# Output and score banks that rotate, and the old output copied in two pieces, in the head loop of an attention layer

## The chip, the cores and the metric

The kernel runs on one core of a Trainium2 chip. The metric is the device time of one execution in microseconds (us), as the median of several runs. The engines are PE (TensorE: matmuls; its weight loads are shown as PEld), DVE (VectorE), ACT (ScalarE), POOL (GpSimd) and SP (SyncE, which issues the DMAs here).

## What is computed

One post-norm transformer layer on x of shape (4, 2048, 256), with 16 heads of 16 channels, rotary positions, and an FFN with int weights and hidden size 768:

```python
qkv = x @ w_qkv + b_qkv
q, k = _rope(q), _rope(k)
attn = softmax(q @ k.T / sqrt(16))          # per batch and head, 2048 x 2048
out = (attn @ v) @ w_out + b_out
x = _layernorm(x + out)
wg, wu, wd = w_gate / 127, w_up / 127, w_down / 127
x = _layernorm(x + (silu(x @ wg.T) * (x @ wu.T)) @ wd.T)
```

## The kernel before

There are three stages: `project` (queries, keys and values, rotary positions), `attend` (the head loop, 80% of the time) and `finish` (output projection, norms, FFN). The change is in `attend` and in `keep`, a step on the SP queue.

`attend` goes over 64 heads (4 batches of 16). Its work on one head h:

- *Maxima.* For softmax each query row needs its largest score. PE computes scores (`scores`, `score_half`, L91) of 128 queries by 1024 keys into one of two tiles `s_ps` (two PSUM banks each); a tile g is computed in halves j = 0 and 1, called scores A and B here. DVE takes the maximum of each tile (`tile_maximum`, L102). There are 32 tiles a head, and they run ahead: while head h is in the loop, its step n computes tile g = (h + 1) * 32 + 10 + n. Tile g waits until DVE has read tile g - 2 (semaphore `s_read`). Of two tiles a head (in steps 10 and 24), ACT copies the first 512 columns to `spared` (L1038) for POOL to fold, and DVE reads only the other 512.
- *Exponentials.* PE computes transposed scores (`scores_t`, L942): product e of 64 in a head (key tile e // 4, 512 queries e % 4), one bank each, called st(e) here. The rows of q hold the maxima, so the product comes out with the maximum taken off. There are ST = 3 banks `st_ps`; product n (counted over all heads) goes to bank n % 3 and waits until exponential n - 3 is done (`exp_done`). ACT takes the exponential into `probs` (L1063).
- *Times v.* `times_v` (L953, called PV here) multiplies probs of a key tile by v (16 channels and a column of ones, so the sum of the exponentials comes with it). It accumulates over the head's 16 key tiles into one bank, `o_ps`. It is issued in halves of 256 queries per key tile, each of four column groups; an fp32 matmul is recorded as two passes, so a half shows as 8 matmuls.
- *Drain.* When the last PV of head h - 1 is done, ACT copies `o_ps` to `sums` in SBUF (`drain`, L1032), behind exponential 4 of head h, and SP stores it (`keep`). The first PV of head h waits for that copy (`sums_out`).

The order on PE is written out in one loop. In each step n = 0 to 31 of head h it issues scores A, st(2n), scores B, one half of PV, and st(2n + 1). So st(2n + 1) runs beside scores A of the next step (they use different rows of the array), and st(2n + 2) beside scores B. PV trails by three steps: steps 0 to 2 issue the last three halves of head h - 1, and step 3 the first half of head h. In the last head the odd st goes ahead of PV.

The order on ACT is exponentials 0, 1, 2, ..., with the drain behind exponential 4 and the copies to `spared` behind exponentials 20 and 48. On SP, a head's turn is: the second stacks of head h + 1, `keep` of head h - 1 (four small DMAs of the sum's row to `spread`, then four stores to `heads`), the first stacks of head h + 2, the inverses of head h - 1 (after DVE's reciprocal at L745, which is issued behind the tile of step 10), and the maxima of head h + 1. The banks in `attend` are 4 for `s_ps`, 3 for `st_ps` and 1 for `o_ps`, all 8.

The functions that the change touches:

Of the kernel before, what the change touches and what calls it, by code (L numbers as in the profile page):

```python
# [7 lines left out]
P = 128  # L8
# [3 lines left out]
BANK = 512  # L12
# [20 lines left out]
def wait(eng, sem, value):  # L33

    if not isinstance(value, int) or value > 0:
        eng.wait_ge(sem, value)
# [687 lines left out]
def unit_steps(t, u, T, D):  # L724

    HD = D // N_HEAD
    QC = T // BANK
    PQ = P // QC

    def keep(sp, h):  # L730

        i = h % 2
        sp.wait_ge(u["sums_out"], h + 1)
        wait(sp, u["inverses_out"][i], h // 2 * 16)
        for c in range(QC):
            sp.dma_start(u["spread"][i][c * PQ:(c + 1) * PQ, :],
                         u["sums"][i][c * 32 + HD:c * 32 + HD + 1, :].rearrange("o (p n) -> o p n", p=PQ)
                         ).then_inc(u["spread_in"][i], 16)
        for c in range(QC):
            sp.dma_start(t["heads"][h * HD:(h + 1) * HD, c * BANK:(c + 1) * BANK],  # L740
                         u["sums"][i][c * 32:c * 32 + HD, :]).then_inc(u["kept"][i], 16)

    def invert(dve, h):
        dve.wait_ge(u["spread_in"][h % 2], (h // 2 + 1) * QC * 16)
        dve.reciprocal(u["spread"][h % 2][:, :], u["spread"][h % 2][:, :]).then_inc(u["inverted"], 1)  # L745

    def inverses(sp, h):
        sp.wait_ge(u["inverted"], h + 1)
        sp.dma_start(t["inverses"][h:h + 1, :].rearrange("h (p n) -> (h p) n", p=P), u["spread"][h % 2][:, :]
                     ).then_inc(u["inverses_out"][h % 2], 16)  # L750

    return dict(keep=keep, invert=invert, inverses=inverses, **u)


def attend(nc, t, w, s, f, u, B, T, D):

    HD = D // N_HEAD
    HEADS = B * N_HEAD
    KT = T // P
    QC = T // BANK  # L760
    QT = T // P
    EXPS = KT * QC
    HALF = BANK // 2
# [5 lines left out]
    ST = 3  # L769
    RING = 4  # L770
# [3 lines left out]
    VM = HD + 1  # L774
# [15 lines left out]
    LEVELS = 9  # L790
    FOLDS = 3 * LEVELS
    LOWEST = -3.0e38
    with ExitStack() as ctx:  # L793
        def sb(name, shape, dt=F32):
            return ctx.enter_context(nc.sbuf_tensor(name, shape, dt))

        def psum(name, shape):
            return ctx.enter_context(nc.psum_tensor(name, shape, F32))
# [5 lines left out]
        out = unit_steps(t, u, T, D)  # L804
        q, k, first_in, second_in = s["q"], s["k"], s["first_in"], s["second_in"]
        probs = [sb(f"probs{i}", [P, T]) for i in range(RING)]
# [5 lines left out]
        larger = sb("larger", [P, BANK // 2])  # L812
        more_top = sb("more_top", [P, QT])
        max_parts = [sb(f"max_parts{i}", [P, PARTS, 32], F16) for i in range(2)]
        st_ps = [psum(f"st_ps{i}", [P, BANK]) for i in range(ST)]
        o_ps = psum("o_ps", [P, BANK])
        TT, KD = WIDE // D, D // P
        p_first = [s_ps[c][:, :].rearrange("p (n d) -> p n d", n=TT) for c in range(2)]

# [4 lines left out]
        o_cleared = sem("o_cleared")  # L824
# [13 lines left out]
        exp_done = sem("exp_done")  # L838
        pv_done = sem("pv_done")
        sums_out, kept, inverses_out = out["sums_out"], out["kept"], out["inverses_out"]  # L840
        spread_in = out["spread_in"]
# [74 lines left out]
        def _(pe):  # L916
# [12 lines left out]
            def scores_t(h, e):  # L929

                if e == 0:
                    pe.wait_ge(second_in[h % 2], (h // 2 + 1) * SECOND_DMAS * 16)
                    pe.wait_ge(max_in[h % 2], (h // 2 + 1) * PARTS * 16)
                kt, c = e // QC, e % QC
                n = h * EXPS + e
                rows = SECOND
                if h == HEADS - 1 and e % 2 == 1:
                    rows = FIRST
                    if e == 1:
                        pe.wait_ge(low_in, (SECOND_DMAS + PARTS) * 16)  # L940
                wait(pe, exp_done, n - ST + 1)
                pe.matmul(st_ps[n % ST][:, :], k[h % 2][rows, kt * P:(kt + 1) * P],  # L942
                          q[h % 2][rows, c * BANK:(c + 1) * BANK], start=True, stop=True).then_inc(st_done, 1)

            def times_v(h, kt, half):

                if half == 0:
                    pe.wait_ge(exp_done, h * EXPS + (kt + 1) * QC)
                    if kt == 0:
                        wait(pe, sums_out, h)  # L950
                at = half * HALF
                for c in range(QC):
                    mm = pe.matmul(o_ps[c * 32:c * 32 + VM, at:at + HALF], t["kept"][:, h, kt, :],  # L953
                                   probs[(h * KT + kt) % RING][:, c * BANK + at:c * BANK + at + HALF],
                                   start=(kt, half) == (0, 0), stop=(kt, half) == (KT - 1, 1), tile_position=(0, c * 32))
                if half == 1:
                    mm.then_inc(pv_done, 1)
# [22 lines left out]
            for g in range(EARLY + 2, MAXES + LEAD):  # L980
                scores(g, 0)
                scores(g, 1)
                if g == MAXES // 2:
                    pe.wait_ge(b_spread, D // P)
                    pe.wait_ge(out_in, 3 * 16)
                    for kd in range(D // P):
                        mm = pe.matmul(st_ps[0][:, 0:D], w["b_v"][:, kd, :], w["w_out"][:, kd, :], start=kd == 0,
                                       stop=kd == D // P - 1)
# [3 lines left out]
            for h in range(HEADS):  # L992
                for n in range(EXPS // 2):
# [9 lines left out]
                    before, half = divmod(n - 3, 2)  # L1003
# [12 lines left out]
        @block.scalar  # L1016
        def _(act):
            act.wait_ge(out_in, 3 * 16)
            act.wait_ge(all_ones, 1)
            for kd in range(D // P):  # L1020
                act.activation(w["b_v"][:, kd, :], w["ones"][:, :], ACT.Identity,
                               scale=w["b_v_cols"][:, kd:kd + 1]).then_inc(b_spread, 1)
            act.wait_ge(ffn_in, len(FFN) * 16)
            for name in FFN:
                act.copy(w[name][:, :, :], w[name][:, :, :].bitcast(I32)).then_inc(floats, 1)

            def drain(h):
                i = h % 2
                act.wait_ge(pv_done, (h + 1) * KT)
                wait(act, kept[i], h // 2 * QC * 16)  # L1030
                wait(act, spread_in[i], h // 2 * QC * 16)
                act.copy(out["sums"][i][:, :], o_ps[:, :]).then_inc(sums_out, 1)  # L1032

            def keep_half(n):

                act.wait_ge(half_done, n + 1)
                wait(act, folded, FOLDS * n)
                act.copy(spared[:, :], s_ps[SPARED[n] % 2][:, 0:BANK]).then_inc(half_kept, 1)  # L1038

            def beside(n):  # L1040

                if n == KEEP_WIDE:
                    act.wait_ge(f["wide_summed"], 1)
                    act.copy(f["wide_count"][:, :], s_ps[0][:, 0:1]).then_inc(f["wide_known"], 1)
                    act.wait_ge(f["wide_known"], 1)
                    act.copy(f["wide_int"][:, :], f["wide_count"][0:1, :]).then_inc(f["wide_known"], 1)
                if n in TAKE_HIGH:
                    steps["take_high"](act, 0, TAKE_HIGH.index(n))
                if n in TAKE_WHOLE:
                    steps["take_whole"](act, 0, TAKE_WHOLE.index(n))  # L1050

            scale = act.alloc_register("exp_scale")
            for h in range(HEADS):
                if h % N_HEAD == 0:
                    b = h // N_HEAD
                    act.reg_load(scale, s["exp_scale"][0:1, b:b + 1].bitcast(I32))
                for e in range(EXPS):
                    kt, c = e // QC, e % QC
                    if c == 0:
                        wait(act, pv_done, h * KT + kt - RING + 1)  # L1060
                    n = h * EXPS + e
                    act.wait_ge(st_done, n + 1)
                    act.activation(probs[(h * KT + kt) % RING][:, c * BANK:(c + 1) * BANK], st_ps[n % ST][:, :],  # L1063
                                   ACT.Exp, scale=scale).then_inc(exp_done, 1)
                    if e == QC and h > 0:
                        drain(h - 1)
                    g = (h + 1) * MAXES + LEAD + e // 2
                    if e % 2 == 0 and g in SPARED:
                        keep_half(SPARED.index(g))
                    if h == HEADS - 1 and e % 2 == 1:  # L1070
                        beside(e // 2)
            steps["load_silu"](act)
            drain(HEADS - 1)

        @block.vector
        def _(dve):
            def clear():
                dve.memset(o_ps[:, :], 0.0).then_inc(o_cleared, 1)
                for i in range(2):
                    dve.memset(head_top[i][:, :], 0.0).then_inc(cleared, 1)  # L1080
                    dve.memset(tile_max[i][:, :, KW:KW + 1], LOWEST).then_inc(cleared, 1)

# [513 lines left out]
```

## Time and profile before

| | |
|---|---|
| time, median of 3 runs (lowest, highest) | 2868.82 us (2866.64, 2869.18) |
| span of the profiled execution, first to last instruction | 2868.1 us |
| part of the span before, in and behind the head loop | 240, 2306, 322 us |
| PE, DVE, ACT, POOL busy, of the span | 98%, 94%, 90%, 49% |
| drains L1032, each | 64, 0.59 us |
| exponentials L1063, each | 4096, 0.60 us |

The profile is of one execution. Its own time is the span of 2868.1 us and what lies around it; the profile gives no other time for it, and the median of the runs is 0.7 us above the span. Busy time counts an instruction from its recorded start to its end, and instructions of one engine overlap, so a busy share near 100% doesn't say that the engine could do no more.

### The profile page before, as it was taken

To read this page: it belongs to the slowest core of one execution; us is meant where nothing else is said; L and a number is where in the kernel's file an instruction comes from. 1 tells how busy PE (TensorE), PEld (TensorE's weight loads), DVE (VectorE), ACT (ScalarE), POOL (GpSimd) and SP (SyncE) were. 2 spreads that over 40 slices of the span, in tenths; PEclk is the share of its full clock that TensorE was granted. 3 is DMA by queue.
4 is the path that set the end of the run, shared out by engine and by line. 5 is a ranking of instruction groups with operands and counts; after the bars stand their busy time and mean duration, and the time that the engine had idled before them with its cause. 6 is when DMAs were issued, how large, how long until landed. Compare 5 with 4: busy or idle time off the path is not lost. (4 is left out here: it accounts for less than half of the span.)

```text
span 2868.1 us, 70575 instructions
## 1 busy us (share of the span) xinstructions
PE 2811.7 (98%) x27022; PEld 862.5 (30%) x27022; DVE 2702.9 (94%) x3088; ACT 2591.9 (90%) x4778; POOL 1416.7 (49%) x4133
## 2 busy tenths in 40 slices
PE   8989999999999999999999999999999999999998
PEld 4531222222222222222222222222222222246665
DVE  7989999999999999999999999999999999947777
ACT  5756999999999999999999999999999999976555
POOL 7851444444444444444444444444444444436553
PEclk9978999999999999999999999999999999999999
DMA  5431111111111111111111111111111111233431
GB/s 194 142 116 28 36 35 36 35 36 35 35 35 35 34 35 36 35 36 36 35 35 35 36 35 35 35 35 36 35 35 36 35 35 35 70 90 92 118 96 38
DMA packets 121519, 146.56 MB, mean 51 GB/s; under 512 B 52832, under 2 KB 87520, under 8 KB 121180
## 3 DMA queue, kind: packets, MB, share of 16 engines
q1 hardware_dynamic: 120892, 142.02, 17.0%
q8 instruction: 214, 3.51, 0.5%
q14 instruction: 125, 1.02, 0.1%
q10 hardware_dynamic: 288, 0.01, 0.0%
HBM read 106.30 MB, written 35.13 MB: 49 GB/s over the span
## 5 line engine op out<-in xcount | busy, mean ns | idle before, releaser
L102 DVE TENSOR_REDUCE tile_max<-s_ps 128x1 f32<-128x1024 f32 (+1 forms) x2048 | 2282.4, 1185 | 8.8 <-PE s_ps L91 2.8
L1063 ACT ACTIVATE probs<-st_ps 128x512 f32<-128x512 f32 x4096 | 2202.2, 601 | 71.0 <-PE st_ps L942 41.1
L953 PE MATMUL o_ps<-probs,kept_v 128*17 128x256 f32 x16384 | 1283.1, 385 | 25.7 <-ACT sums L1032 25.7
L91 PE MATMUL s_ps<-k,q 64*128 64x512 f16 x4096 | 1266.2, 386 | 11.0 <-DVE tile_max L102 9.2
L942 PE MATMUL st_ps<-q,k 64*128 64x512 f16 x4096 | 1249.5, 382 | 1.1 <-ACT probs L1063 0.8
L1198 POOL TENSOR_TENSOR larger<-spared 128x256 f32<-128x256 f32 x1107 | 342.8, 310 | 675.6 <-ACT spared L1038 598.5
L953 PEld LDWEIGHTS o_ps<-probs,kept_v 128*17 128x17 f32 x16384 | 273.6, 95 | 852.2 <-ACT probs L1063 445.6
L942 PEld LDWEIGHTS st_ps<-q,k 64*128 64x128 f16 x4096 | 256.1, 94 | 902.0 <-ACT probs L1063 842.3
L1207 POOL TENSOR_TENSOR spared<-spared,larger 128x256 f32<-128x256 f32 x984 | 318.4, 324 | 81.9
L1200 POOL TENSOR_SCALAR larger<-larger 128x256 f32<-128x256 f32 x1107 | 261.4, 236 | 96.8
L91 PEld LDWEIGHTS s_ps<-k,q 64*128 64x128 f16 x4096 | 250.2, 94 | 50.4 <-DVE tile_max L102 46.5
L1512 POOL TENSOR_TENSOR h_low<-hidden,h_high 128x512 f16<-128x512 f32 x96 | 112.6, 1180 | 148.4 <-ACT h_high L1388 148.3
L1400 ACT ACTIVATE silu<-g_ps 128x512 f32<-128x512 f32 x96 | 57.1, 594 | 102.9 <-PE g_ps L1327 102.9
L1182 POOL TENSOR_TENSOR more_top<-tile_max 128x16 f32<-128x16 f32 x64 | 13.9, 217 | 225.1 <-DVE tile_max L102 225.0
L256 PE MATMUL s_ps<-x_t,w_qkv 128*128 128x512 f32 x256 | 117.1, 612 | 6.3 <-DMA x_t<-in_x_t 6.3
L1436 DVE SCALAR_TENSOR_TENSOR hidden<-u_ps,hidden_factor,silu 128x512 f32<-128x512 f32 x96 | 70.1, 745 | 47.0 <-PE u_ps L1327 34.5
L439 POOL TENSOR_TENSOR raw<-raw,cos 128x512 f32<-128x512 f32 x64 | 80.7, 1275 | 17.8 <-ACT raw L317 17.8
L1327 PE MATMUL s_ps<-w_down_half,h_high 128*128 128x256 f16 x384 | 84.8, 273 | 1.6 <-POOL h_low L1512 1.6
L1327 PE MATMUL s_ps<-w_down_half,h_low 128*128 128x256 f16 x384 | 84.8, 273 | 0.0
L317 ACT ACTIVATE raw<-s_ps,bias_qk 128x512 f32<-128x512 f32 x64 | 43.2, 684 | 36.7 <-PE s_ps L256 36.1
L445 POOL TENSOR_TENSOR parts<-raw,parts 128x1024 f16<-128x1024 f32 x32 | 68.3, 2135 | 14.1 <-ACT parts L310 14.1
L1327 PE MATMUL g_ps<-x_high,w_gate_half 128*128 128x512 f16 x192 | 72.8, 379 | 1.4 <-PEq L793 1.4
(119 smaller groups left out, 1625.3 us busy)
## 6 DMA issues: line engine op xcount, KB each, us to landing
q<-q_parts SPq DMA_DIRECT2D x193, 128.0 KB
k<-k_parts SPq DMA_DIRECT2D x193, 128.0 KB
x_t<-in_x_t SPq DMA_DIRECT2D x16, 512.0 KB, 7.2
q_parts<-parts SPq DMA_DIRECT2D x32, 256.0 KB, 2.6
k_parts<-parts SPq DMA_DIRECT2D x32, 256.0 KB, 2.6
heads_out<-sums SPq DMA_DIRECT2D x256, 32.0 KB, 2.1
kept_v<-heads_out SPq DMA_DIRECT2D x16, 512.0 KB, 6.1
kept_v<-inverses_out SPq DMA_DIRECT2D x32, 256.0 KB
```

The lines of the kernel that those rows point to most:

```text
L91: mm = pe.matmul(s["s_ps"][g % 2][:, j * BANK:(j + 1) * BANK], s["q"][h % 2][rows, r // KW * P:(r // KW + 1) * P], s["k"][h % 2][rows, at: ...
L102: dve.tensor_reduce(s["tile_max"][h % 2][:, r // KW, r % KW:r % KW + 1], s["s_ps"][g % 2][:, columns], AX.X, ALU.max).then_inc(s["s_read"], 1)
L256: mm = pe.matmul(qk_ps[m][:, :], w_qkv[:, kd, m * P:(m + 1) * P], x[:, kd, :], start=kd == 0, stop=kd == KD - 1)
L439: pool.tensor_tensor(raw[i][:, m, :], raw[i][:, m, :], cos[:, c * CH:(c + 1) * CH], ALU.mult).then_inc(cosined, 1)
L942: pe.matmul(st_ps[n % ST][:, :], k[h % 2][rows, kt * P:(kt + 1) * P], q[h % 2][rows, c * BANK:(c + 1) * BANK], start=True, stop=True).then ...
L953: mm = pe.matmul(o_ps[c * 32:c * 32 + VM, at:at + HALF], t["kept"][:, h, kt, :], probs[(h * KT + kt) % RING][:, c * BANK + at:c * BANK + a ...
L1063: act.activation(probs[(h * KT + kt) % RING][:, c * BANK:(c + 1) * BANK], st_ps[n % ST][:, :], ACT.Exp, scale=scale).then_inc(exp_done, 1)
L1198: pool.tensor_tensor(more, b, a, ALU.subtract).then_inc(folded, 1)
L1200: pool.tensor_scalar(more, more, -LOWEST, 0.0, ALU.min, ALU.max).then_inc(folded, 1)
L1207: pool.tensor_tensor(a_or_top, a, more, ALU.add).then_inc(folded, 1)
L1327: mm = pe.matmul(to, stationary, moving, start=first and n == 0, stop=last and n == len(pairs) - 1)
L1512: pool.tensor_tensor(h_low[:, m, :], hidden[:, m, :], h_high[:, m, :], ALU.subtract).then_inc(h_low_done, 1)
```

## The change

The output bank is no longer a bank of its own. There are four banks, `bank_ps0` to `bank_ps3`; at any time three are the ring for transposed scores and one holds the output. Head h > 0 takes for its output the bank in which st(4) stood, once exponential 4 is done. The old output bank joins the ring after it is copied: st(7) goes to the bank of st(5) (and so waits for exponential 5, where it waited for exponential 4), and st(8) goes to the old output bank and waits for the copy. The copy is made in two pieces of 256 columns, the first behind exponential 4 and the second behind exponential 5, each counting `sums_out` up by one; SP waits for both. The last head's copy is in two pieces too.

```diff
     def keep(sp, h):
         i = h % 2
-        sp.wait_ge(u["sums_out"], h + 1)
+        sp.wait_ge(u["sums_out"], 2 * (h + 1))
...
+    HANDED = QC
+    ring = list(range(ST))
+    sum_bank, score_bank = [ST], []
+    for h in range(HEADS):
+        if h > 0:
+            sum_bank.append(ring[(h * EXPS + HANDED) % ST])
+        for e in range(EXPS):
+            if h > 0 and e == HANDED + ST:
+                first, second = (h * EXPS + e) % ST, (h * EXPS + e + 1) % ST
+                ring[first], ring[second] = ring[second], sum_bank[h - 1]
+            score_bank.append(ring[(h * EXPS + e) % ST])
...
-        st_ps = [psum(f"st_ps{i}", [P, BANK]) for i in range(ST)]
-        o_ps = psum("o_ps", [P, BANK])
+        banks = [psum(f"bank_ps{i}", [P, BANK]) for i in range(ST + 1)]
+        st_ps = [banks[i] for i in score_bank]
+        o_ps = [banks[i] for i in sum_bank]
...
-                wait(pe, exp_done, n - ST + 1)
-                pe.matmul(st_ps[n % ST][:, :], k[h % 2][rows, kt * P:(kt + 1) * P],
+                if h > 0 and e == HANDED + ST:
+                    pe.wait_ge(exp_done, n - ST + 2)
+                elif h > 0 and e == HANDED + ST + 1:
+                    pe.wait_ge(sums_out, 2 * h)
+                else:
+                    wait(pe, exp_done, n - ST + 1)
+                pe.matmul(st_ps[n][:, :], k[h % 2][rows, kt * P:(kt + 1) * P],
...
                 if half == 0:
-                    pe.wait_ge(exp_done, h * EXPS + (kt + 1) * QC)
-                    if kt == 0:
-                        wait(pe, sums_out, h)
+                    handed = kt == 0 and h > 0
+                    pe.wait_ge(exp_done, h * EXPS + (HANDED + 1 if handed else (kt + 1) * QC))
...
-                    mm = pe.matmul(o_ps[c * 32:c * 32 + VM, at:at + HALF], t["kept"][:, h, kt, :],
+                    mm = pe.matmul(o_ps[h][c * 32:c * 32 + VM, at:at + HALF], t["kept"][:, h, kt, :],
...
-            def drain(h):
-                i = h % 2
-                act.wait_ge(pv_done, (h + 1) * KT)
-                wait(act, kept[i], h // 2 * QC * 16)
-                wait(act, spread_in[i], h // 2 * QC * 16)
-                act.copy(out["sums"][i][:, :], o_ps[:, :]).then_inc(sums_out, 1)
+            def drain(h, half):
+                i, at = h % 2, half * HALF
+                if half == 0:
+                    act.wait_ge(pv_done, (h + 1) * KT)
+                    wait(act, kept[i], h // 2 * QC * 16)
+                    wait(act, spread_in[i], h // 2 * QC * 16)
+                act.copy(out["sums"][i][:, at:at + HALF], o_ps[h][:, at:at + HALF]).then_inc(sums_out, 1)
...
-                    if e == QC and h > 0:
-                        drain(h - 1)
+                    if e in (HANDED, HANDED + 1) and h > 0:
+                        drain(h - 1, e - HANDED)
...
-            drain(HEADS - 1)
+            for half in range(2):
+                drain(HEADS - 1, half)
...
-                dve.memset(o_ps[:, :], 0.0).then_inc(o_cleared, 1)
+                dve.memset(o_ps[0][:, :], 0.0).then_inc(o_cleared, 1)
```

## Rows read from the trace of the kernel before

**Rows 1.** The page: its span, and each engine's busy time, share and instructions.

```profile
span 2868.1 us, 70575 instructions
...
PE 2811.7 (98%) x27022; PEld 862.5 (30%) x27022; DVE 2702.9 (94%) x3088; ACT 2591.9 (90%) x4778; POOL 1416.7 (49%) x4133
```

**Rows 2.** Windows: the head loop; stretch and its length, then busy time by engine.

```profile
240.00:2546.00 2306.00, 2279.13 (x24509) 548.91 (x24507) 2269.80 (x2185) 2266.43 (x4282) 1092.87 (x3897) 1.00 0.13 37
```

**Rows 3.** Timeline of ACT: two drains; start, duration, engine, line, operation.

```profile
1029.18 0.59 ACT L1032 COPY sums<-o_ps 128x512 f32<-128x512 f32 x1
...
1065.12 0.59 ACT L1032 COPY sums<-o_ps 128x512 f32<-128x512 f32 x1
```

**Rows 4.** Timeline of PE: one undisturbed step, PV to PV.

```profile
1044.29 0.63 PE L953 MATMUL o_ps<-probs,kept_v 128*17 128x256 f32 x8
...
1045.07 0.38 PE L942 MATMUL st_ps<-q,k 64*128 64x512 f16 x1
...
1045.38 0.63 PE L953 MATMUL o_ps<-probs,kept_v 128*17 128x256 f32 x8
```

**Rows 5.** Timeline of DVE, two narrow stretches around the drain; merged, duration to last end.

```profile
1028.76 2.35 DVE L102 TENSOR_REDUCE tile_max<-s_ps 128x1 f32<-128x1024 f32 x2
...
1029.89 2.48 DVE L102 TENSOR_REDUCE tile_max<-s_ps 128x1 f32<-128x1024 f32 x2
```

**Rows 6.** Timeline of DVE: reads between the short ones, and behind step 10.

```profile
1018.48 20.16 DVE L102 TENSOR_REDUCE tile_max<-s_ps 128x1 f32<-128x1024 f32 x18
1038.55 0.24 DVE L745 RECIPROCAL spread<-spread 128x16 f32<-128x16 f32 x1
1038.81 15.50 DVE L102 TENSOR_REDUCE tile_max<-s_ps 128x1 f32<-128x1024 f32 x14
...
1038.81 2.46 DVE L102 TENSOR_REDUCE tile_max<-s_ps 128x1 f32<-128x1024 f32 x2
```

**Rows 7.** Timeline of ACT, narrow stretches: exponential 4, then 5 with 6.

```profile
1028.71 0.59 ACT L1063 ACTIVATE probs<-st_ps 128x512 f32<-128x512 f32 x1
...
1029.65 1.12 ACT L1063 ACTIVATE probs<-st_ps 128x512 f32<-128x512 f32 x2
```

**Rows 8.** Waits: engine and line, whom it waited for, total, times, longest.

```profile
PE o_ps L953 <- ACT sums L1032: 25.7, 63, 0.4
```

**Rows 9.** Timeline of PE at the drain: second pair of step 3 to step 4.

```profile
1029.13 0.38 PE L91 MATMUL s_ps<-k,q 64*128 64x512 f16 x1
1029.92 0.63 PE L953 MATMUL o_ps<-probs,kept_v 128*17 128x256 f32 x8 [0.41 <-ACT sums L1032]
1030.48 0.39 PE L942 MATMUL st_ps<-q,k 64*128 64x512 f16 x1
...
1030.71 0.38 PE L942 MATMUL st_ps<-q,k 64*128 64x512 f16 x1
```

**Rows 10.** Timelines of PEld and ACT: loads that waited for DVE and for ACT.

```profile
1028.90 0.09 PEld L91 LDWEIGHTS s_ps<-k,q 64*128 64x128 f16 x1
...
1038.91 0.63 ACT L1063 ACTIVATE probs<-st_ps 128x512 f32<-128x512 f32 x1
...
1039.58 0.09 PEld L942 LDWEIGHTS st_ps<-q,k 64*128 64x128 f16 x1 [0.26 <-ACT probs L1063]
```

**Rows 11.** Groups by line and shape, ACT reading PSUM: count, busy us, mean ns.

```profile
L317 ACT ACTIVATE raw<-s_ps,bias_qk 128x512 f32<-128x512 f32 x64 | 43.2, 684 | 36.7 <-PE s_ps L256 36.1
...
L1032 ACT COPY sums<-o_ps 128x512 f32<-128x512 f32 x64 | 37.9, 592 | 0.0
...
L1044 ACT COPY wide_count<-s_ps 128x1 f32<-128x1 f32 x1 | 0.2, 191 | 0.0
```

**Rows 12.** Timeline of SP's queue: the sum's row, four DMAs.

```profile
1029.80 2.46 SPq L736 DMA_DIRECT2D spread<-sums  x4
```

**Rows 13.** Timeline of PEld at the last head's boundary.

```profile
2508.43 0.09 PEld L942 LDWEIGHTS st_ps<-q,k 64*128 64x128 f16 x1 [0.17 <-ACT probs L1063]
2509.00 0.16 PEld L953 LDWEIGHTS o_ps<-probs,kept_v 128*17 128x17 f32 x8 [0.48 <-issue]
```

More of the change, by code:

```diff
@@ L1062, in _ @@
                     act.wait_ge(st_done, n + 1)
-                    act.activation(probs[(h * KT + kt) % RING][:, c * BANK:(c + 1) * BANK], st_ps[n % ST][:, :],
+                    act.activation(probs[(h * KT + kt) % RING][:, c * BANK:(c + 1) * BANK], st_ps[n][:, :],
                                    ACT.Exp, scale=scale).then_inc(exp_done, 1)
-                    if e == QC and h > 0:
-                        drain(h - 1)
+                    if e in (HANDED, HANDED + 1) and h > 0:
+                        drain(h - 1, e - HANDED)
                     g = (h + 1) * MAXES + LEAD + e // 2
```

## The prediction

> **What bounds the kernel now.** I read the page first: PE, DVE and ACT are all busy for 90% or more of the span [rows 1], so the busy shares don't name a bound. Split by stage, the 2306 us of the head loop show PE 2279, DVE 2270 and ACT 2266 us [rows 2], with the granted clock at 1.00, the upper of its two levels. What bounds it has to be read from the distances between starts. One head takes 1065.12 - 1029.18 = 35.94 us from drain to drain [rows 3].
>
> - PE's undisturbed step (two pairs of score matmuls, eight passes of probs times v) repeats every 1045.38 - 1044.29 = 1.09 us [rows 4]; I use 1.094. 32 steps are 35.0 us, 0.9 less than a head.
> - DVE reads one 1024-column tile per step. Two back-to-back reads span 2.35 us with 1.22 for the last [rows 5], so the distance is 1.13. DVE is thus slower than PE's step by 0.037 us. The row of 18 reads runs 20.16 us, the last being the short one of 0.68 us: 19.48 over 17 distances, where 17 x 1.131 is 19.23, so 0.25 us idle; the 14 reads behind it give 15.50 - 0.68 = 14.82 against 13 x 1.131 = 14.70, so 0.12 [rows 6]. DVE idles only about 0.37 us per head. That is all that any change of PE or ACT can win: 0.37 x 62 = 23 us.
> - ACT, when it has a backlog, starts exponentials 0.49 apart (1.12 less the last one's 0.63) [rows 7], against 0.547 per exponential in PE's step. It catches up after each copy and isn't the bound, although its busy time (which counts overlapping tails) looks full.
>
> So DVE is nearly the bound, PE follows, and PE's stalls count where they drain the lead that PE has over DVE (two score tiles). The one stall at the head's boundary is the wait for the drain: 63 times, 25.7 us in the list of waits [rows 8]. That is 0.41 each, counted from the modelled ends of the matmuls before. By starts, the second pair of step 3 is at 1029.13 and PV at 1029.92 [rows 9], 0.79 apart where the undisturbed step has 1045.38 - 1045.07 = 0.31 [rows 4]. So PE loses 0.48 to 0.50 us.
>
> **The change part by part.** Step n issues st(2n) with scores A and B, one PV half, and st(2n+1), which forms the first pair of the next step. All times are for the boundary at 1029.
>
> 1. *PV of the new head in a bank of its own.* It no longer waits for the drain (removed: the wait of [rows 8]), but for exponential 4, whose bank it takes. Exponential 4 starts at 1028.71 and lasts 0.59 [rows 7], so it ends at 1029.30. From the end of an exponential to PE's load are 1039.58 - (1038.91 + 0.63) = 0.04 to 0.05 us [rows 10]: 1029.35. PE would come to PV by itself at 1029.11 + 0.31 = 1029.42. No stall; without this cover each 0.1 us of a later exponential would be paid.
>
> 2. *The copy in two pieces of 256 columns.* No copy of this size is in the trace. The whole copy lasts 0.592, a one-column copy from PSUM 0.191 [rows 11], so a column costs about 0.785 ns and 256 columns less save 0.20: a piece lasts 0.39. The next exponential starts 1029.65 - 1029.18 = 0.47 behind the whole copy [rows 3, 7], so 0.27 behind a piece. Bounds: below, 0.19 for the one column; above, the whole copy's 0.59, and farthest the 0.684 of the PSUM read with a bias [rows 11]. I take 0.39 and 0.27, as the form and the engine are the same and only the length differs.
>
> 3. *New waits.* st(7) now needs exponential 5 rather than 4, and st(8) needs both pieces. ACT: piece one at 1029.18, exponential 5 at 1029.45, ending 1029.45 + 0.63 = 1030.08 (the duration that the exponential behind a copy has in [rows 10]); with 0.05 the first pair of step 4 can go at 1030.13. Today it goes at 1030.48 [rows 9]. Piece two starts 0.48 behind exponential 5 (the drain is 1029.18 - 1028.71 = 0.47 behind exponential 4 today [rows 3, 7]), at 1029.93, and ends at 1030.32; with 0.05 st(8) can go at 1030.37. PE comes to it at 1030.13 + 0.23 = 1030.36. Today it goes at 1030.71 [rows 9]. Queued behind st(7) and st(8) on PE are scores A and B, so DVE's next tile waits too. Step 4 starts 0.33 to 0.34 us earlier, and of the 0.50 stall about 0.16 stays. Exponentials 6 and 7 start at about 1030.20 and 1030.7; st(9) and st(10), due from about 1031.23 on, find them finished.
>
> 4. *What DVE makes of it.* Today the read of step 4 starts at 1029.89 + 2.48 - 1.23 = 1031.14 [rows 5], 0.43 behind its second pair at 1030.71. DVE was free at 1029.89 + 1.13 = 1031.02, so 0.12 to 0.13 idle plus 0.01 in the slower distance behind it. After the change the tile is there at 1030.37 + 0.43 = 1030.80, and DVE has no idle: 0.14 won. PE is then 0.22 ahead. The lead grows by 0.037 a step, but is capped: before the drain, scores A waits for DVE, whose read started 1.13 before the one at 1028.76 and took 1.22, so ended at 1028.85; PE's load for scores A is at 1028.90 [rows 10]; the lead there is 1029.89 - (1029.13 + 0.43) = 0.33 [rows 5, 9]. At step 10, where POOL's share of a tile gives DVE a short read, the lead is today 6 x 0.037 = 0.22, and will be at the cap, 0.33: another 0.10 or so, spent on the idle time there. That idle time is 1038.81 + 2.46 - 1.23 = 1040.04, less 1038.81, less 1.13 = 0.10, plus 0.01 and some hundredths behind the reciprocal [rows 6]. I take 0.09. The idle 0.11 behind the second short read (step 24) stays, since PE is at its cap before it in both kernels.
>
> A rule weighed here: the Trainium skill, page "Perfetto Trace Analysis", section "Optimizing Scalar/DVE Operations", states a data-access overhead per instruction (about 51 ns of ScalarE time on PSUM) and advises larger operations where the engine is saturated, but splitting where an unsaturated engine causes bubbles elsewhere. With ACT saturated the extra piece would cost an estimated 0.05 us a head by that page, some 3 us slower; with ACT unsaturated the second half of the rule holds and the gain below stands.
>
> 5. *Sync queue.* The DMAs of the sums wait for both pieces: they start at 1030.37 instead of 1029.80 [rows 12] and run 2.46 us. The first to need them is DVE's reciprocal at 1038.55 [rows 6]. Everything on this queue behind them (the sums' stores, the next head's first stacks, the maxima) moves 0.6 us; the stores follow directly, and the reads of the stacks belong to the next head but one. I cost it at nothing; if the cover were gone it would cost at most the 0.6 per head.
>
> 6. *The ends.* In the last head DVE has no tiles and the odd st goes ahead of PV, so PE waits for st(7) with PV behind it. Today st(7) goes at 2508.43 and PV at 2509.00 [rows 13]; with a piece and exponential 5 first, st(7) goes at about 2509.2 and PV at 2509.5: 0.5 lost once. The last drain costs one more fixed part, 0.07. The rotation itself adds no instruction.
>
> **The sum.** 0.14 + 0.09 = 0.23 us for each of 62 boundaries is 14.3; less 0.6 at the ends is 13.7. The profiled execution has a span of 2868.1; the median of the runs, 2868.8, is 0.7 above it. 2868.1 - 13.7 + 0.7 = 2855.1 us, 0.48% less.
>
> **The rivals.**
>
> - *The lead isn't kept.* DVE wins only the 0.14 at the boundary, because PE waits for ACT or DVE before step 10. For it: PE and ACT are coupled through three score banks. Against it: the steady distances. 62 x 0.14 - 0.6 = 8.1: 2860.7. Chance 0.14.
> - *All of DVE's idle time goes.* If the lead could also cover step 24, 0.37 x 62 - 0.6 = 22: 2846.5. Against it is the cap. Chance 0.06.
> - *Pieces nearly as dear as a whole copy.* st(8) goes at 1029.71 plus start-to-start and duration of a piece (0.66 in my sum). If they come to 0.90 or more, less than 0.10 is won per head, and nothing measurable remains; with the whole copy's 0.47 + 0.59 = 1.06, st(8) goes at 1030.77, 0.06 later than today: 2868.8 + 3.7 + 0.6 = 2873.1. Up to there it is no change within 0.2% (which is about what a measurement of this kernel tells from none). Chance 0.10, centre 2868.
> - *Slower.* The same place with the upper price: at 0.684, and a distance longer by the same 0.09 (0.56), st(8) goes at 1029.71 + 0.56 + 0.68 = 1030.95, 0.24 late, and all of it becomes DVE idle time: 62 x 0.24 + 0.6 = 15.5 slower: 2884.3. It ends slower from a sum of 1.00 on, and by over 0.2% from 1.08. For it: the waits st(7) and st(8) now stand ahead of both score tiles on PE. Against it: the same copy's 0.592. Chance 0.05.
> - *ACT is the bound after all.* Two pieces occupy 2 x 0.27 = 0.54 against 0.47: 0.07 x 63 = 4.4 slower, 2873.2; if pieces were dearer, beyond 0.2%. Against it: distances of 0.49 after each copy where 0.547 is the pace. Chance 0.02. It is what the page's first rule would give here.
>
> **How the numbers follow.** The forecast has 0.63. Its own range, from pieces of 0.33 to 0.50 us and a share of step 10 between 0.05 and 0.12, is 2852.5 to 2858.5. For 8 in 10 the range takes in the first rival and stops short of the others: 2851.5 to 2862.5. Faster: 0.63 + 0.14 + 0.06 = 0.83; same 0.10; slower 0.07.
>
> **What would show it.** Distance from drain to drain 35.70 instead of 35.93. Pieces of 0.39 us; exponential 5 starting 0.27 behind the first; the new head's PV 0.31 behind its pair; the first pair of step 4 some 0.71 behind that PV instead of 0.56, held by exponential 5; DVE's read of step 4 at 1.13 behind the one before. The list of waits loses PE o_ps behind sums. The row of 18 reads shrinks by 0.14 and that of 14 by 0.05 to 0.10. Wrong would make it: pieces over 0.5 us, a wait on st(8) that costs more than 0.05 from the copy's end to the load, or DVE's reads becoming longer with the new banks.

## The result and the profile after

The changed kernel takes 2851.31 us (median of 5 runs, 2850.52 to 2853.68) where the kernel before takes 2868.82 (5 runs, 2866.64 to 2869.18). The ratio is 0.9945 with a 95% interval of 0.9933 to 0.9957: 17.5 us or 0.55% less, forecast 13.7. The median is 0.2 us under the low end of the stated range (2851.5 to 2862.5).

The page of the changed kernel, against [rows 1]:

```profile
span 2851.4 us, 70576 instructions
...
PE 2817.0 (99%) x27022; PEld 876.9 (31%) x27022; DVE 2690.6 (94%) x3088; ACT 2582.0 (91%) x4842; POOL 1416.3 (50%) x4133
...
L1049 ACT COPY sums<-bank_ps 128x256 f32<-128x256 f32 x128 | 49.8, 390 | 0.0
```

(The last line is from its groups by line and shape.) The busy shares hardly move, as they showed no bound before. Where the time went is seen in the distance from one drain to the next. ACT's timeline of the changed kernel, at the same head as [rows 3, 7]:

```profile
1023.30 0.38 ACT L1049 COPY sums<-bank_ps 128x256 f32<-128x256 f32 x1
1023.55 0.63 ACT L1080 ACTIVATE probs<-bank_ps 128x512 f32<-128x512 f32 x1
1024.04 0.40 ACT L1049 COPY sums<-bank_ps 128x256 f32<-128x256 f32 x1
...
1058.96 0.38 ACT L1049 COPY sums<-bank_ps 128x256 f32<-128x256 f32 x1
```

1058.96 - 1023.30 = 35.66 us a head, where it was 35.93 to 35.94: 0.27 less. Over the 61 such distances that is 0.27 x 61 = 16.5 of the 16.7 us by which the span is shorter. The pieces last 0.38 and 0.40, and exponential 5 starts 0.25 behind the first.

PE's timeline there, against [rows 9]:

```profile
1023.24 0.38 PE L91 MATMUL s_ps<-k,q 64*128 64x512 f16 x1
1023.55 0.63 PE L969 MATMUL bank_ps<-probs,kept_v 128*17 128x256 f32 x8
1024.23 0.39 PE L959 MATMUL bank_ps<-q,k 64*128 64x512 f16 x1
...
1024.50 0.39 PE L91 MATMUL s_ps<-k,q 64*128 64x512 f16 x1
```

and its weight loads, with what they waited for:

```profile
1024.23 0.09 PEld L959 LDWEIGHTS bank_ps<-q,k 64*128 64x128 f16 x1 [0.55 <-ACT probs L1080]
...
1024.49 0.09 PEld L959 LDWEIGHTS bank_ps<-q,k 64*128 64x128 f16 x1 [0.17 <-ACT sums L1049]
```

PV follows its pair after 0.31, as in an undisturbed step [rows 4]; the wait of [rows 8] is gone from the list. In its place st(7) waits for exponential 5 and st(8) for the second piece. That last wait costs little: the second pair of step 4 starts 0.26 to 0.27 behind the first one, where 0.23 is usual. From second pair to second pair PE takes 1024.50 - 1023.24 = 1.26 where it took 1.58.

DVE's timeline, against [rows 6]:

```profile
1012.59 20.02 DVE L102 TENSOR_REDUCE tile_max<-s_ps 128x1 f32<-128x1024 f32 x18
1032.53 0.24 DVE L745 RECIPROCAL spread<-spread 128x16 f32<-128x16 f32 x1
1032.70 15.45 DVE L102 TENSOR_REDUCE tile_max<-s_ps 128x1 f32<-128x1024 f32 x14
...
1032.70 2.41 DVE L102 TENSOR_REDUCE tile_max<-s_ps 128x1 f32<-128x1024 f32 x2
```

The row of 18 reads, in whose middle the drain stands, is 20.16 - 20.02 = 0.14 shorter. From the reciprocal to the read behind it are 0.17 instead of 0.26, 0.09 less, and the row of 14 is 0.05 shorter, all of it between its first two reads. Together, and before rounding, they are the 0.27. So all of the gain is idle time of DVE: half at the boundary (0.14 by these rows, 0.134 before rounding), and half around the reciprocal, seven and eight steps later.

### The profile page after: what moved, and what is told of

The parts are those of the page before. It is cut to its first block and busy times, and to the rows that moved or that the text cites. A ratio compares the mean times of both kernels' runs of the same rounds, so it can differ in the third digit from the quotient of the medians.

```text
span 2851.4 us, 70576 instructions
## 1 busy us (share of the span) xinstructions
PE 2817.0 (99%) x27022; PEld 876.9 (31%) x27022; DVE 2690.6 (94%) x3088; ACT 2582.0 (91%) x4842; POOL 1416.3 (50%) x4133
## 5 line engine op out<-in xcount | busy, mean ns | idle before, releaser
L1080 ACT ACTIVATE probs<-bank_ps 128x512 f32<-128x512 f32 x4096 | 2198.5, 604 | 63.7 <-PE bank_ps L959 40.7
L969 PE MATMUL bank_ps<-probs,kept_v 128*17 128x256 f32 x16384 | 1283.1, 385 | 0.0
L959 PE MATMUL bank_ps<-q,k 64*128 64x512 f16 x4096 | 1248.1, 382 | 5.2 <-ACT probs L1080 1.5
L959 PEld LDWEIGHTS bank_ps<-q,k 64*128 64x128 f16 x4096 | 269.3, 93 | 917.5 <-ACT probs L1080 846.1
L969 PEld LDWEIGHTS bank_ps<-probs,kept_v 128*17 128x17 f32 x16384 | 271.7, 95 | 805.7 <-issue 414.5
L91 PEld LDWEIGHTS s_ps<-k,q 64*128 64x128 f16 x4096 | 259.4, 94 | 50.5 <-DVE tile_max L102 46.5
L439 POOL TENSOR_TENSOR raw<-raw,cos 128x512 f32<-128x512 f32 x64 | 80.6, 1273 | 17.5 <-ACT raw L317 17.5
```

What stands on the lines that cost most here:

```text
L91: mm = pe.matmul(s["s_ps"][g % 2][:, j * BANK:(j + 1) * BANK], s["q"][h % 2][rows, r // KW * P:(r // KW + 1) * P], s["k"][h % 2][rows, at: ...
L439: pool.tensor_tensor(raw[i][:, m, :], raw[i][:, m, :], cos[:, c * CH:(c + 1) * CH], ALU.mult).then_inc(cosined, 1)
L959: pe.matmul(st_ps[n][:, :], k[h % 2][rows, kt * P:(kt + 1) * P], q[h % 2][rows, c * BANK:(c + 1) * BANK], start=True, stop=True).then_inc( ...
L969: mm = pe.matmul(o_ps[h][c * 32:c * 32 + VM, at:at + HALF], t["kept"][:, h, kt, :], probs[(h * KT + kt) % RING][:, c * BANK + at:c * BANK ...
```

## The experiments

The times of each are set against runs of the kernel before on the same chip (2867.7 to 2868.2 as median).

**The banks rotate, the copy stays whole**

```diff
...
-                act.copy(out["sums"][i][:, at:at + HALF], o_ps[h][:, at:at + HALF]).then_inc(sums_out, 1)
...
+                act.copy(out["sums"][i][:, :], o_ps[h][:, :]).then_inc(sums_out, 1)
...
-                    if e in (HANDED, HANDED + 1) and h > 0:
-                        drain(h - 1, e - HANDED)
+                    if e == HANDED and h > 0:
+                        drain(h - 1)
...
```

The waits of st(8) and of SP count one copy a head instead of two.

> The banks rotate as in the changed kernel, but the old output is copied whole (512 columns) behind exponential 4. Theory (DVE's idle time decides, PE's stall is only paid beyond the lead): exponential 5 starts 0.47 behind the copy and ends at 1.10 after its start, so the first pair of step 4 loads at 1.14 to 1.15 after the drain's start (before 1.29, changed 0.93) and the second pair starts near 1.38 (before 1.52, changed 1.20). DVE's read of step 4 then has no idle time: 0.137 won at the boundary and about 0.03 at step 11, 0.17 a head, less 0.3 at the ends: 2857 to 2860 us. Rival 'the rotation alone does it, the pieces add nothing': 2851 as the changed kernel. Rival 'the pieces alone do it': 2867 to 2869.

Measured: 2858.51 us, ratio 0.9970 (0.9959 to 0.9981). 35.78 us from drain to drain, 0.15 less than before. Two drains in ACT's timeline, and PE's behind the first:

```profile
1023.33 0.59 ACT L1048 COPY sums<-bank_ps 128x512 f32<-128x512 f32 x1
...
1059.11 0.59 ACT L1048 COPY sums<-bank_ps 128x512 f32<-128x512 f32 x1
```

```profile
1023.58 0.63 PE L969 MATMUL bank_ps<-probs,kept_v 128*17 128x256 f32 x8
1024.47 0.39 PE L959 MATMUL bank_ps<-q,k 64*128 64x512 f16 x1 [0.27 <-ACT probs L1079]
...
1024.70 0.38 PE L91 MATMUL s_ps<-k,q 64*128 64x512 f16 x1
```

The pairs stand where expected, 1.14 and 1.37 behind the drain's start. Read for read, the rotation alone wins the whole boundary part of DVE's idle time (0.134 before rounding) and 0.016 behind the reciprocal, where 0.03 was expected. The pieces are worth the other 0.12 a head, none of it at the boundary: they start PE's next step 0.17 earlier, and that lead is spent later. So neither part gives the whole gain alone, and both rivals fall.

**Pieces, fixed bank**

```diff
...
-                        wait(pe, sums_out, h)
+                        wait(pe, sums_out, 2 * h)
...
-                act.copy(out["sums"][i][:, :], o_ps[:, :]).then_inc(sums_out, 1)
...
+                act.copy(out["sums"][i][:, at:at + HALF], o_ps[:, at:at + HALF]).then_inc(sums_out, 1)
...
-                    if e == QC and h > 0:
-                        drain(h - 1)
+                    if e in (QC, QC + 1) and h > 0:
+                        drain(h - 1, e - QC)
...
```

> The kernel before with its fixed output bank, but the copy in two pieces of 256 columns, behind exponentials 4 and 5; the new head's first PV waits for both. Theory: the second piece ends 0.742 + 0.403 = 1.145 after the first one's start, PV loads at 1.26 instead of 0.705, 0.55 later, and all of it becomes idle time of DVE: 62 x 0.55 = 34 slower, 2900 to 2906 us. Rival 'exponential 5 starting earlier is what helps, the bank does not matter': 2868 or less. Rival 'PE has slack at the boundary': under 2880.

Measured: 2902.69 us, ratio 1.0118 (1.0102 to 1.0133), 35 us slower; 34 expected. PE's timeline and the list of waits:

```profile
1040.34 0.38 PE L91 MATMUL s_ps<-k,q 64*128 64x512 f16 x1
1041.68 0.63 PE L953 MATMUL o_ps<-probs,kept_v 128*17 128x256 f32 x8 [0.97 <-ACT sums L1033]
```

```profile
PE o_ps L953 <- ACT sums L1033: 60.9, 63, 1.0
```

PV stands 1.34 behind its pair instead of 0.79. The same two pieces that help with the rotation cost 0.55 a head without it (36.48 us from drain to drain), because the exponential between them then stands between PE and the bank. Both rivals fall.

**Each piece as dear as a whole copy**

```diff
...
-                act.copy(out["sums"][i][:, at:at + HALF], o_ps[h][:, at:at + HALF]).then_inc(sums_out, 1)
+                act.copy((again if half else out["sums"])[i][:, :], o_ps[h][:, :]).then_inc(sums_out, 1)
```

> The changed kernel, but each of the two copies reads and writes all 512 columns (the second one goes to a tile that nobody uses). This is the case in which a piece costs as much as a whole copy: 0.592 each, 0.466 to the next exponential. Theory: the first pair of step 4 loads at 1.15 after the first copy's start, the second copy starts at 0.95 and ends at 1.56, st(8) loads at 1.60 and its pair starts 0.08 later than in the kernel before (1.52): 0.08 x 62 = 5, plus 0.8 in the last head, so 2872 to 2876 us, slower than the kernel before although PV still does not wait for the copy. Rival 'the cost of the copies is covered, only PV's wait for the drain counted': 2851 to 2860.

Measured: 2877.42 us, ratio 1.0031 (1.0020 to 1.0042): slower than before, 1.4 us above the range that was expected. ACT and PE in its timeline (the second group is PE's):

```profile
1029.93 0.59 ACT L1050 COPY sums<-bank_ps 128x512 f32<-128x512 f32 x1
1030.40 0.63 ACT L1081 ACTIVATE probs<-bank_ps 128x512 f32<-128x512 f32 x1
1030.89 0.62 ACT L1050 COPY again<-bank_ps 128x512 f32<-128x512 f32 x1
```

```profile
1030.19 0.63 PE L970 MATMUL bank_ps<-probs,kept_v 128*17 128x256 f32 x8
1031.08 0.39 PE L960 MATMUL bank_ps<-q,k 64*128 64x512 f16 x1 [0.27 <-ACT probs L1081]
...
1031.56 0.39 PE L91 MATMUL s_ps<-k,q 64*128 64x512 f16 x1
```

PV doesn't wait for a copy here either, yet the second pair stands 1.63 behind the drain's start, 0.10 later than before (1030.71 - 1029.18 = 1.53), and the head takes 36.05 us, 0.115 more. So the gain hangs on the price of the pieces, as the prediction's rival on dear pieces had it. That rival put the delay at 0.06 and the loss at 4.3 us; they measure 0.10 and 9.8.

**The copy for POOL split too**

```diff
...
-                act.copy(spared[:, :], s_ps[SPARED[n] % 2][:, 0:BANK]).then_inc(half_kept, 1)
...
+                act.copy(spared[:, at:at + HALF], s_ps[SPARED[n] % 2][:, at:at + HALF]).then_inc(half_kept, 1)
...
-                    g = (h + 1) * MAXES + LEAD + e // 2
-                    if e % 2 == 0 and g in SPARED:
-                        keep_half(SPARED.index(g))
+                    g = (h + 1) * MAXES + LEAD + (e + 1) // 2
+                    if g in SPARED:
+                        keep_half(SPARED.index(g), 1 - e % 2)
...
```

The waits of PE and POOL for the copy count two pieces.

> The changed kernel, and the copy of 512 score columns for POOL is split in the same manner: 256 columns behind the odd exponential before and 256 behind the exponential where it stood whole. Theory: the exponential that PE waits for there (the one behind the copy) starts no earlier, since both pieces still stand ahead of it (0.49 + 0.25 + 0.49 + 0.25 against 0.49 + 0.49 + 0.47), so DVE's idle time of 0.07 at step 11 and 0.11 at step 24 stays: no gain, 0 to 0.04 per copy slower, 2850 to 2856 us. Rival 'shorter pieces on ACT help wherever they stand': up to 0.18 x 62 = 11 less, 2840 to 2848.

Measured: 2860.63 us, ratio to before 0.9975 (0.9964 to 0.9986), so 8 to 9 us slower than the changed kernel and above the expected range. 35.79 a head, 0.127 more, where 0 to 0.08 was expected. The timelines of ACT and PE:

```profile
1033.88 0.37 ACT L1057 COPY spared<-s_ps 128x256 f32<-128x256 f32 x1
1034.13 0.61 ACT L1082 ACTIVATE probs<-bank_ps 128x512 f32<-128x512 f32 x1
1034.62 0.39 ACT L1057 COPY spared<-s_ps 128x256 f32<-128x256 f32 x1
1034.87 1.62 ACT L1082 ACTIVATE probs<-bank_ps 128x512 f32<-128x512 f32 x3
```

```profile
1034.36 0.38 PE L91 MATMUL s_ps<-k,q 64*128 64x512 f16 x1
...
1035.57 0.39 PE L91 MATMUL s_ps<-k,q 64*128 64x512 f16 x1
```

The exponential that PE waits for, the one behind the second piece, starts 0.05 later than behind a whole copy (9.50 against 9.45 behind the drain's start), and PE's next second pair comes 1035.57 - 1034.36 = 1.21 behind the last one instead of 1.15. Splitting gained nothing, as the exponential that holds PE up is not the one between the pieces but the one behind both, and two pieces take more of ACT than one copy (2 x 0.25 against 0.47). The rival falls.

**No short reads, both kernels**

```diff
-    SPARED = [h * MAXES + r for h in range(2, HEADS) for r in ROWS][:-1]
+    SPARED = []
```

> The kernel before without the short reads: ACT copies nothing for POOL, POOL folds nothing, and DVE reads all 1024 columns of every tile. Theory: DVE's work per head is 32 x 1.131 + 0.18 + 0.18 = 36.55 us, PE is always at the cap of its lead, and the only idle time of DVE is what the drain's stall leaves beyond the lead, 0.137: 36.69 a head, 2913 to 2917 us. To be compared with the next run.

> The changed kernel without the short reads, as the run before. Theory: DVE never idles, 36.55 us a head, so this is 0.137 x 62 = 8.5 us less than the kernel before without short reads: 2904 to 2908. The change then wins only its boundary part, not the 0.13 at step 11. Rival 'PE's stall counts in full' (0.36 less stall per head): 22 less. Rival 'the gain does not depend on DVE': 16 to 17 less, as in the change itself. Rival 'DVE alone is the bound': 0.

Measured: 2900.39 us (1.0112, 1.0096 to 1.0129) and 2896.90 us (1.0101, 1.0084 to 1.0118), both below their expected ranges. The timed runs put them 3.5 apart, with intervals that overlap, so the times alone don't tell them apart. The distances from drain to drain are sharper, 36.47 and 36.39, the kernel before first:

```profile
1013.21 0.59 ACT L1032 COPY sums<-o_ps 128x512 f32<-128x512 f32 x1
...
1049.68 0.59 ACT L1032 COPY sums<-o_ps 128x512 f32<-128x512 f32 x1
```

```profile
1037.86 0.38 ACT L1049 COPY sums<-bank_ps 128x256 f32<-128x256 f32 x1
...
1074.25 0.38 ACT L1049 COPY sums<-bank_ps 128x256 f32<-128x256 f32 x1
```

That is 0.08 a head and 5 us in all. (The two profiled spans, 2909.7 and 2895.1 us, lie further apart, but 10.1 us of that stand ahead of the first drain, at 283.75 and 273.64.) None of the rivals fits (22, 16 to 17, or 0), and it also falls short of the 0.137 of the theory. PE's timeline of the kernel before without short reads shows why, with DVE's at the same place:

```profile
1049.68 0.38 PE L91 MATMUL s_ps<-k,q 64*128 64x512 f16 x1
1050.42 0.63 PE L953 MATMUL o_ps<-probs,kept_v 128*17 128x256 f32 x8 [0.36 <-ACT sums L1032]
...
1051.21 0.38 PE L91 MATMUL s_ps<-k,q 64*128 64x512 f16 x1
```

```profile
1050.45 2.42 DVE L102 TENSOR_REDUCE tile_max<-s_ps 128x1 f32<-128x1024 f32 x2
```

Its drain starts at 1049.68, together with scores B; in the kernel before it starts 0.05 behind them (1029.18 and 1029.13). Where PE has been paced by DVE for many steps, st and with it ACT's exponentials run a little ahead of the score tiles (here the st of this pair starts at 1049.64, its scores at 1049.68), and a stall that ACT causes is shorter by just that: from second pair to second pair 1.53 here, 1.58 before. DVE's idle time at the boundary is 0.08 instead of 0.134. The level was also misjudged, by 10 us: 36.39 a head is 32 x 1.131 = 36.19 and 0.20 for the reciprocal and the transposition together, where 0.36 was expected.

**The short read two steps later, both kernels**

```diff
-    ROWS = (2, 20)
+    ROWS = (2, 22)
-    INVERT = 10
+    INVERT = 12
```

> The kernel before with its second short read (and the reciprocal behind it) two steps later, in step 12 instead of step 10. Theory: PE's lead over DVE grows from nothing at the drain by 0.037 us a step and is what decides the idle time behind the short read. Two steps more give 0.074 more lead, still under the cap of 0.32 (0.23 + 0.07 = 0.30), so DVE's idle time behind the short read shrinks by 0.074: 35.86 us a head instead of 35.93, 62 x 0.074 = 4.6 less, 2863 to 2864 us. Rival 'the position of the short read does not matter': 35.93 a head, 2867.7.

> The same edit in the changed kernel. Theory: there PE's lead is at its cap from step 7 on, so two steps more give nothing: 35.66 us a head, 2850 to 2853 us, and the change is worth 35.86 - 35.66 = 0.19 to 0.20 a head here, 12 us in all, of which 0.137 is the boundary's part as before. Rival 'the part at the short read is something else than lead': the difference between this and the run before stays at 0.27 a head, 16 to 17 us.

Measured: 2862.69 us (0.9980, 0.9971 to 0.9989; 2863 to 2864 expected), 35.86 a head; and 2851.90 us (0.9944, 0.9931 to 0.9958), 35.66 to 35.67 a head. By the heads the change is worth 0.19 here, as the theory had it, and not the 0.27 of the rival. DVE's timelines, the kernel before first:

```profile
1039.39 0.24 DVE L745 RECIPROCAL spread<-spread 128x16 f32<-128x16 f32 x1
1039.58 13.23 DVE L102 TENSOR_REDUCE tile_max<-s_ps 128x1 f32<-128x1024 f32 x12
```

```profile
1033.31 0.24 DVE L745 RECIPROCAL spread<-spread 128x16 f32<-128x16 f32 x1
1033.49 13.19 DVE L102 TENSOR_REDUCE tile_max<-s_ps 128x1 f32<-128x1024 f32 x12
```

Two more steps of lead take 0.07 from the idle time behind the reciprocal before (0.26 to 0.19) and nothing in the changed kernel (0.17 to 0.18), where the lead is at its cap. Moving the short read alone, without the change, wins 5.5 us, about a third of the change's gain.

**The last head without the rotation**

```diff
...
-            sum_bank.append(ring[(h * EXPS + HANDED) % ST])
+            sum_bank.append(ring[(h * EXPS + HANDED) % ST] if h < HEADS - 1 else sum_bank[h - 1])
...
+                    if kt == 0 and h == HEADS - 1:
+                        pe.wait_ge(sums_out, 2 * h)
...
+                    if e == HANDED and h == HEADS - 1:
+                        drain(h - 1, 0)
+                        drain(h - 1, 1)
...
```

> The changed kernel, but in the last head the banks do not rotate: its PV stays in the output bank of head 62 and waits for the copy, both pieces of which stand behind exponential 4; st(7) waits for exponential 4 again. Theory: the last distance from drain to drain returns from 38.56 to 38.05 to 38.15 us (0.4 to 0.5 less), and nothing else changes; too little to be seen in the time of the runs. Rival 'the longer last head has another cause': the distance stays at 38.5.

Measured: one run, 2851.24 us. The last two drains in ACT's timeline, in this run and in the changed kernel:

```profile
2489.34 0.65 ACT L1051 COPY sums<-bank_ps 128x256 f32<-128x256 f32 x2
...
2527.36 0.63 ACT L1051 COPY sums<-bank_ps 128x256 f32<-128x256 f32 x2
```

```profile
2491.09 0.37 ACT L1049 COPY sums<-bank_ps 128x256 f32<-128x256 f32 x1
...
2529.64 0.63 ACT L1049 COPY sums<-bank_ps 128x256 f32<-128x256 f32 x2
```

From drain 62 to drain 63 it is 2527.36 - 2489.34 = 38.02 us, where the changed kernel has 38.55 and the kernel before 38.05. The 0.5 lost in the last head is the price of the new order there; the time as a whole doesn't tell.

## Why the prediction was right

The direction and the mechanism were right. The gain was larger than forecast, by 3 us in the span and by 4 in the medians, which put the time just under the range. The term that was too small is the share of step 10: 0.09 forecast, 0.13 measured.

- *DVE is nearly the bound, with 0.37 idle per head, and that is all there is to win.* The bound is right: all of the gain is found in distances of DVE, and with DVE filled (no short reads) the change is worth 0.08 a head instead of 0.27. The 0.37 is too small. It is the idle time inside the two rows of reads, and leaves out the idle time between the reciprocal and the read behind it, which is 0.09: DVE idled some 0.45 a head. The rival in which all of it goes put that gain some 5 us too low.
- *Step 1, PV no longer waits.* Right: 0.31 behind its pair.
- *Step 2, the price of a piece.* Right: 0.38 and 0.40 for 0.39, and 0.25 for 0.27. With whole copies in their place the changed kernel is 9.8 us slower than the one before, so this was the term that carried the sign. Of the rule of the Trainium skill, "Perfetto Trace Analysis", "Optimizing Scalar/DVE Operations", the second half, that splitting may help where an engine that isn't saturated holds up others, shows at the drain, where PE waited for the exponential between the pieces. The same engine holds PE up at the copy for POOL too, and there splitting cost 0.127 a head, so the rule's condition alone doesn't decide it. No run here has ACT saturated, so its first half isn't tested.
- *Step 3, the new waits.* Right: behind the drain's start st(7) loads at 0.93 (0.95 worked out) and st(8) at 1.19 to 1.20 (1.19). PE would have come to st(8) by itself 0.03 to 0.04 earlier, where the prediction had 0.01.
- *Step 4, the boundary's 0.14.* Right: 0.14 by the rows, 0.134 before rounding.
- *Step 4, the share of 0.09 at step 10.* The mechanism was right and the size was off: it measures 0.13. Of it, 0.09 is the lead that the prediction counted; it is all spent behind the reciprocal, where the idle time that the prediction put at "some hundredths" was 0.09. The other 0.04 was not in the prediction. These are PE's second pairs of steps 10 and 12 with ACT's copy for POOL, the kernel before and then the changed one:

```profile
1037.28 0.38 PE L91 MATMUL s_ps<-k,q 64*128 64x512 f16 x1
...
1038.44 0.59 ACT L1038 COPY spared<-s_ps 128x512 f32<-128x512 f32 x1
...
1039.59 0.39 PE L91 MATMUL s_ps<-k,q 64*128 64x512 f16 x1
```

```profile
1031.16 0.38 PE L91 MATMUL s_ps<-k,q 64*128 64x512 f16 x1
...
1032.29 0.59 ACT L1055 COPY spared<-s_ps 128x512 f32<-128x512 f32 x1
...
1033.44 0.39 PE L91 MATMUL s_ps<-k,q 64*128 64x512 f16 x1
```

The changed kernel's PE reaches the cap of its lead in step 8 and is paced by DVE from there to step 11 (its second pairs come 1.13 apart instead of 1.09). As in the run without short reads, ACT's copy then starts earlier against the pairs: 1032.29 - 1031.16 = 1.13 behind the second pair of step 10, where it was 1038.44 - 1037.28 = 1.16. PE's second pair of step 12 comes 2.28 behind that of step 10 instead of 2.32 (2.31 by the rounded rows). In the run with the whole copy, where nothing paces PE before step 10, that distance is 2.32 as before, and the 0.04 is missing. 0.04 x 61 = 2.5 us is most of the 3 us between forecast and span.
- *Step 24 keeps its 0.11.* Right: the distance behind the first read after the second short one is 1.23 in both.
- *Step 5, the Sync queue.* Right: it starts its four DMAs at 1024.47, 1.17 behind the drain instead of 0.62, and comes to the inverses at 1033.04, behind the reciprocal; the list of waits shows no new wait for its DMAs.
- *Step 6, the ends.* Right: 0.5 lost in the last head. The distance before it, in which DVE has no reads from step 22 on, won 0.41 (41.46 to 41.04) and not 0.23. The run with the whole copy has 41.04 there too, although its PE stalls 0.17 longer at the boundary, so why it is 0.41 stays open.

What would have made it wrong, a piece over 0.5 us, was tried; that DVE's reads become longer with the new banks did not happen (1.131 apart in both).

## What to carry to other kernels

When three engines run within a few per cent of each other, a stall of one is worth only what it drains from the slowest one's queue: find the slowest by start-to-start distances, count its idle time per period (the gaps beside its small operations too), and follow the lead of the engine in front of it from the stall to the next place where it is spent. Splitting a copy is worth its second fixed cost where the instruction that the stalled engine waits for can go between the pieces, and whatever needs the last piece comes about when that piece is done. With a buffer to rotate, that is so (st(8) goes only 0.03 to 0.04 us later for the second piece); without it the same split cost 35 us. A stall costs less when the engine in front has time to win its lead back before the slowest one's next short piece of work, so the distance between the two is a knob of its own.

## What the runs showed that was not expected

- An ACT copy from PSUM of 256 columns lasts 0.38 to 0.40 us and one of 512 lasts 0.59; behind them the next exponential starts 0.25 and 0.47 later. The 256 columns more cost 0.21 us in both, before rounding.
- DVE's two small operations per head cost less where DVE never idles and has no short reads: 0.20 us for both, read as 36.39 - 32 x 1.131, where their distances to the next read are 0.17 and 0.18 in the changed kernel. The runs don't separate the two conditions.
- An engine that is held back by a slower one shortens the stalls that a third one causes. The drain's stall is 0.05 us shorter with DVE filled, and the second pair behind the copy for POOL follows the one before it after 1.15 instead of 1.22 in the changed kernel. Of that 0.07, 0.04 is PE's pace, as the one before it comes 1.13 instead of 1.09 behind its own, and over both steps 0.04 is won.
